# Attention with a gated mixture of experts: rows, K, Q and V in natural order at the begin, 44 unread products, the third group's loads moved ahead

## The reference

```python
def _L0_xattn_ref(q, k, v, mask, Wq, bq, Wk, bk, Wv, bv):   # 16 heads of 16
    Qh, Kh, Vh = split(q @ Wq + bq), split(k @ Wk + bk), split(v @ Wv + bv)
    scores = jnp.einsum('bqhd,bkhd->bhqk', Qh, Kh) / jnp.sqrt(jnp.float32(10.0))
    scores = jnp.where(mask[:, None, None, :] == 0, jnp.float32(-1000000000.0), scores)
    return jnp.einsum('bhqk,bkhd->bqhd', jax.nn.softmax(scores, axis=-1), Vh).reshape(B, S, D)
x = x + jnp.tanh(g_xattn[0]) * _L0_xattn_ref(_layernorm(x), ctx_1024, ctx_1024, mask, ...)
x = x + jnp.tanh(g_ffn[0]) * _L0_ffn_ref(_layernorm(x), Wg, W1, W2, W3)
```

## Time and profile before

| | |
|---|---|
| median of 3 runs | 827.55 us (827.4 to 828.44) |
| the profiled execution: its time | 823.12 us |
| its span, first to last instruction | 821.4 us |
| TensorE (PE) busy | 754.5 us, 92% |
| VectorE (DVE) | 564.9 us, 69% |
| ScalarE (ACT) | 513.2 us, 62% |
| GpSimd (POOL) | 368.7 us, 45% |
| mean granted TensorE clock | 0.960 |

### The profile page before, as it was taken

The page is one execution under the profiler, slowest core; times in us unless marked ns, Lnnn a source line. Parts: engine busy times, 40 slices in busy tenths (PEclk is TensorE's granted clock), DMA queues, the critical chain, the costliest instruction groups (busy, mean ns, idle before and its releaser), DMA issues. The chain is left out here.

```text
span 821.4 us, 24913 instructions
## 1 busy us (share of the span) xinstructions
PE 754.5 (92%) x9614; PEld 630.9 (77%) x9614; DVE 564.9 (69%) x1450; ACT 513.2 (62%) x1001; POOL 368.7 (45%) x761
## 2 busy tenths in 40 slices
PE   6799999999999999999998712999999999999995
PEld 3688888888888888888886601678889898888985
DVE  7577787778777877788778798584754747374440
ACT  3366777777777777767756675456565555656632
POOL 6233534453435443544322230627465474847416
PEclk8999999999999999999999955999999999999998
DMA  5543335543554345444332270535445363524314
GB/s 185 153 132 119 126 101 174 172 153 114 159 173 156 124 146 175 142 142 139 129 113 83 79 208 25 159 112 82 115 81 117 66 135 113 89 46 86 34 20 52
DMA packets 76773, 97.08 MB, mean 118 GB/s; under 512 B 8264, under 2 KB 55880, under 8 KB 76616
## 3 DMA queue, kind: packets, MB, share of 16 engines
q1 hardware_dynamic: 63120, 77.52, 29.5%
q0 software_dynamic: 12288, 17.05, 12.8%
q10 hardware_dynamic: 1248, 0.92, 0.3%
HBM read 52.37 MB, written 25.72 MB: 95 GB/s over the span
## 5 line engine op out<-in xcount | busy, mean ns | idle before, releaser
L746 DVE TENSOR_REDUCE m_sb<-a_ps 128x4 f32<-128x512 f32 x256 | 164.3, 684 | 53.2 <-PE a_ps L1047 51.6
L569 ACT ACTIVATE p_t<-b_ps 128x512 f32<-128x512 f32 x252 | 141.8, 589 | 66.0 <-PE b_ps L1055 63.7
L1047 PE MATMUL a_ps<-k_st,q_st 31*128 31x128 f32 x2048 | 148.7, 283 | 7.1 <-DVE m_sb L746 3.1
L1466 POOL DMA_INDIRECT out<-y,idx_add x64 | 100.4, 1569 | 114.5 <-ACT y L1527 93.2
L1047 PEld LDWEIGHTS a_ps<-k_st,q_st 31*128 31x128 f32 x2048 | 124.8, 186 | 32.3 <-issue 23.5
L1055 PE MATMUL b_ps<-q_st,k_st 32*128 32x128 f32 x1984 | 143.8, 283 | 0.0
L482 POOL TENSOR_TENSOR x<-o_n,x_res 128x256 f32<-128x256 f32 x63 | 46.3, 735 | 186.9 <-DVE o_n L836 168.5
L1055 PEld LDWEIGHTS b_ps<-q_st,k_st 32*128 32x128 f32 x1984 | 120.2, 186 | 0.0
L1727 DVE TENSOR_TENSOR act_h<-act_h,bank 128x512 f32<-128x512 f32 x64 | 44.0, 688 | 80.3 <-PE bank L1871 77.5
L1871 PE MATMUL bank<-x_hi,w_hi 128*128 128x512 f32 x248 | 97.6, 394 | 0.4 <-ACT act_h L1515 0.4
L1871 PE MATMUL bank<-x_lo,w_hi 128*128 128x512 f32 x248 | 96.6, 390 | 0.0
(11 more groups left out here) (299 smaller groups left out, 1742.4 us busy)
## 6 DMA issues: line engine op xcount, KB each, us to landing
w<-in_w_t SPq DMA_DIRECT2D x24, 512.0 KB, 4.7
rows_scratch<-xg SPq DMA_DIRECT2D x16, 528.0 KB, 3.4
x_in<-in_x SPq DMA_DIRECT2D x16, 512.0 KB, 4.7
c_t<-in_ctx_t SPq DMA_DIRECT2D x16, 512.0 KB, 4.4
k_st<-k_val SPq DMA_DIRECT2D x64, 128.0 KB
q_st<-q_val SPq DMA_DIRECT2D x64, 128.0 KB, 2.4
x_res<-in_x SPq DMA_DIRECT2D x16, 512.0 KB, 3.8
out<-x SPq DMA_DIRECT2D x16, 512.0 KB, 3.3
```

The source lines that it names most:

```text
L569: act.activation(p_t[b.s % 2][:, 4 * r:4 * r + 4, :], ps[q % 2][:].rearrange("p (h s) -> p h s", s=P), ACT.Exp, scale=SCALE).then_inc(exp_ ...
L746: dve.tensor_reduce(m_sb[b.s % 2][:, 4 * q:4 * q + 4], a_ps[q % 2][:].rearrange("p (h s) -> p h s", s=P), AX_X, ALU.max).then_inc(max_done, 1)
L1047: mm = pe.matmul(a_ps[i][:, t * P:(t + 1) * P], q_st[p][r:r + A_K, t, tok], k_st[p][r:r + A_K, t, tok], start=True, stop=True)
L1466: pool.indirect_dma_start(out[:, :], bass.IndirectOffsetOnAxis(ap=idx_add[e % 2][:, st:st + 1], axis=0), y[st][:], None, compute_op=ALU.ad ...
```

## The change

It touches the begin of attention and the first group's four batches.

- TensorE: 44 unread products instead of 20; the first group's fronts in the order 0 to 7; then the second group's rows (fronts 0 and 1), to `b_ps`, which are free until the third batch. The first group's batches then make the second group's fronts 2 to 7, two each in the first three batches, none in the fourth but for the third group's front 0.
- VectorE: the first group's `c_lo` (`first_context_lo`), GpSimd's until now, behind the bias row; `xn_rest` ahead of `make_k`; the second group's `xn_rest` ahead of the loop, its `make_k` in the first batch, its `make_v` in the third. One of the two fills of `q_st` goes to GpSimd.
- ScalarE: the second group's `context_hi` ahead of `q_out`, its rows' scaling behind it, and its `xn_t_out` ahead of the loop. `q_out` of the first group waits for `k_done` too, since both count up the same `f_free`. The second group's `q_out` stand both in the second batch.
- GpSimd: `context_lo` of the second group ahead of the fill of `v_aug[1]`.
- SP: the second group's mask and the third group's x are issued ahead of `stack_k`, the third group's context and mask behind `stack_q`, instead of in the first batch.

```diff
-WARM = 20
+WARM = 44
...
         if first(g):
             return (f_ps, m_ps, a_ps[0], a_ps[1], b_ps[0], b_ps[1], pv_ps, o_ps)[u]
+        if second(g) and u < 2:
+            return b_ps[u]
         return f_ps
...
             mask_row(Group(0, 0, NG))
+            load_mask(Group(0, 1, NG))
+            load_x(Group(1, 0, NG))
             stack_k(Group(0, 0, NG))
             stack_q(Group(0, 0, NG))
-            load_mask(Group(0, 1, NG))
+            load_c(Group(1, 0, NG))
+            load_mask(Group(1, 0, NG))
...
-                    if first(g):
-                        load_c(g.on(2))
-                        load_x(g.on(2))
-                        load_mask(g.on(2))
                     residual(g)
...
                 pool.memset(k_st[p][:], 0.0).then_inc(s_ones, 1)
+            pool.memset(q_st[1][:], 1.0).then_inc(s_ones, 1)
...
-            context_lo(Group(0, 0, NG))
             ln1(Group(0, 1, NG))
+            context_lo(Group(0, 1, NG))
             pool.memset(v_aug[1][:], 0.0).then_inc(s_zero, 1)
-            context_lo(Group(0, 1, NG))
...
                     f_wait(g, 4 + m)
+                    if first(g):
+                        act.wait_ge(k_done, m + 1)
...
-            normalise(Group(0, 1, NG), range(GB))
+            context_hi(Group(0, 1, NG))
             for m in range(KD):
                 q_out(g, m)
-            context_hi(Group(0, 1, NG))
+            normalise(Group(0, 1, NG), range(GB))
+            for k in range(KD):
+                xn_t_out(Group(0, 1, NG), k)
...
+            def first_context_lo():
+
+                for k in range(KD):
+                    dve.wait_ge(ch_done, k + 1)
+                    dve.tensor_tensor(c_lo[0][:, k, :], c_t[:, k, :], c_hi[0][:, k, :].bitcast(F32), ALU.subtract).then_inc(cl_done, 1)
...
+            first_context_lo()
             weights_rest(0)
             stats(Group(0, 1, NG), range(GB))
             weights_rest(1)
+            for k in range(KD):
+                xn_rest(g, k)
             for m in range(KD):
                 make_k(g, m)
-            for k in range(KD):
-                xn_rest(g, k)
...
-            v_ones(1)
+            for k in range(KD):
+                xn_rest(Group(0, 1, NG), k)
...
-            for u in (2, 3, 0, 1, 4, 5, 6, 7):
-                if u == 0:
-                    pe.wait_ge(w["s_id"], 2)
+            pe.wait_ge(w["s_id"], 2)
+            for u in range(8):
                 front(Group(0, 0, NG), u)
+            for u in range(KD):
+                front(Group(0, 1, NG), u)
...
-                if b.j == 0 and first(g):
-                    front(g.on(1), 0)
-                front(g.on(1), 2 * b.j + 1)
+                if not first(g):
+                    front(g.on(1), 2 * b.j + 1)
+                elif b.j < 3:
+                    front(g.on(1), 2 * b.j + 2)
```

More of the change, by code:

```diff
@@ L279, in first, with second @@
         return 2 * g.k + g.p == 0
+    def second(g):
+        return 2 * g.k + g.p == 1
     def at_last(b, g, j):
@@ L629, in step @@
                 exp(b.back(2), 1)
-                if b.j == 0:
-                    if first(g):
-                        xn_t_out(f, 0)
+                if b.j == 0 and not first(g):
                     xn_t_out(f, 1)
-                if b.j == 2:
+                if b.j == 1 and first(g):
+                    q_out(f, 0)
+                if b.j == 2 and not first(g):
                     q_out(f, 1)
@@ L692, in _ @@
             dve.memset(warm[:], 0.0).then_inc(s_warm, 1)
-            for p in range(2):
-                dve.memset(q_st[p][:], 1.0).then_inc(s_ones, 1)
+            dve.memset(q_st[0][:], 1.0).then_inc(s_ones, 1)
             def stats(g, ts):
@@ L892, in step @@
                 maximum(b, 1)
-                if b.j == 0:
-                    if first(b.group):
-                        xn_rest(f, 0)
+                if b.j == 0 and not first(b.group):
                     xn_rest(f, 1)
-                if b.j == 1:
+                if b.j == 0 and first(b.group):
+                    make_k(f, 0)
+                if b.j == 1 and not first(b.group):
                     make_k(f, 1)
-                if b.j == 3:
+                if b.j == 2 and first(b.group):
+                    v_ones(1)
+                    make_v(f, 0)
+                if b.j == 3 and not first(b.group):
                     make_v(f, 1)
@@ L906, in step @@
                 if b.j == 0:
-                    make_k(f, 0)
+                    make_k(f, 1 if first(b.group) else 0)
                     stats(b.group.on(2), (0, 1))
@@ L911, in step @@
                 if b.j == 2:
-                    make_v(f, 0)
+                    make_v(f, 1 if first(b.group) else 0)
                 if b.j == 3:
@@ L995, in front @@
                     pass
+                elif second(g) and u < 2:
+                    pe.wait_ge(q_done, KD)
                 elif u == 0:
```

20 lines of the change are left out of this document (10 added, 10 removed).

## The result

| | before | after |
|---|---|---|
| median, us (runs) | 827.47 (4: 826.82 to 828.44) | 820.11 (4: 818.94 to 820.87) |
| ratio, 95% interval | | 0.9912, 0.9900 to 0.9925 |
| profiled execution, us (span) | 823.12 (821.4) | 819.81 (818.1) |
| first scores | 27.78 | 24.50 |
| fifth batch's scores | 54.87 | 47.62 |

A forecast was written before the change was run, and what follows sets the result against it. TensorE is full in attention's loop, so an earlier start carries through. First scores 4.5 us earlier plus 3.4 from the first four batches make 7.9, taken off the median 827.55: 819.7 us, range 815.5 to 823.5.

The forecast's parts named there:

- the walk: TensorE's new order stepped through in time: rows until 13.5, first scores at 23.3, fifth batch at 47.0 us.
- Part 1: LayerNorm's scales: c_lo moved off GpSimd ends a collision, so xn starts 2.0 us earlier, at 9.9; moved memset does nothing.
- Part 2: VectorE's queue at the begin: w_lo_k done at 12.15, xn_lo at 16.1, k_val at 17.6, before Q's second front ends.
- the rival sum of 7.7: Alternative to 7.9: w_lo_q and w_lo_v lose up to 0.2 us each against GpSimd's second scales; no chance given.
- Part 3: Unread products, 20 to 44: end at 12.46, hold TensorE 0.5 us, keep full clock for K, rows and Q.
- Part 4: TensorE's begin in the new order: first scores at 23.3 instead of 27.78, 4.5 us earlier; q_st's transfer ready at 23.0.
- Part 5: SP's queue: the moved loads go out without open waits, near 13.8, ahead of k_done; cost 0, bound 0 to 1.
- Part 6: First group's four batches: first scores to fifth batch takes 23.7 us instead of 27.09, 3.4 us gained.
- the chance of 0.12: Rival, first batches: TensorE's idle pieces let the clock fall again, gain only 5 to 6.5 us, some 822; chance 0.12.
- The loads' rival: Rival at the stacking: K's and Q's transfers queue behind x_in and c_t, scores 2 to 4 us later, about 823; chance 0.06.
- the gain was not taken back: Rival: SP's stacking or ScalarE's normalise sets the fifth batch at 53 or later, 826 to 827.5; chance 0.04.
- the products did not hold PE at half clock throughout: Slower case at the begin: the 44 products stay at half clock, first scores at 38.4, time 834.8; chance 0.04.

The follow-up runs named there:

- e1: After with 20 unread products instead of 44; median 820.74 us, ratio to before 0.9926.
- e9: After with K ahead of the rows on TensorE and k_val ahead of xn_lo on VectorE; median 821.63 us, ratio 0.9935.
- e10: e3 with 32 unread products instead of 44, measured on another chip; median 816.54 us, ratio to before there 0.9903.
- e3: After with the fill of q_st[1] back on VectorE; median 820.02 us, ratio to before 0.9922.
- e6: e3 with the first half of the first group's K laid out from ScalarE's queue instead of SP's; median 820.88 us, ratio 0.9923.
- e7: After with the first group's two c_lo subtractions back on GpSimd; median 821.65 us, ratio to before 0.9940.
- e4: After with the second group's mask and third group's x, context and mask loads at their old places; median 821.05 us, ratio 0.9928.
- e13: After's new batches behind before's begin (20 products, K first, old loads, subtractions and fills), on another chip; median 826.93 us, ratio 1.0036.
- e2: Before with 44 unread products and nothing else changed; median 827.83 us, ratio to before 1.0008.
- e5: After with the first group's four batches as in before, the new begin kept; median 824.95 us, ratio 0.9980.

## Why the prediction was right

The forecast held: 819.7 against 820.11, within its range. Two terms in it were mis-sized: the first scores' by 1.2 too much, the batches' by 0.6 too little. The second makes up for half of the first, and the two hang together: in the walk K's first front of the second group waits for xn_lo until 24.95, and since the scores come late, that wait is gone (the front starts at 25.59). Where PE does not wait for q_st, as in e1, e9 and e10, the wait is there (0.48) and the batches take 23.63 to 23.67, the 23.7 of the forecast. That the sum is off by 0.4 only is chance beyond that: the number of products at half clock alone moves the rows by up to 1.1 (12.43 in e3, 13.57 in e6).

- **Part 1, the scales: half right.** Predicted 2.0, measured 1.1 (xn at 10.77, not 9.9). "The q_st memset that moves to POOL does nothing for this" is the step that failed. It shifts the next fill to 6.74 to 8.53, and DVE's first step of the scales takes 1.18 in place of 0.17; e3 shows it by taking the move back. The step has one input, and POOL's instruction only writes. The line of the Trainium skill (SBUF — State Buffer, "Who interferes with whom") that the prediction used is about instructions with two inputs; the same section names `tensor_scalar` among those that can take both pairs of ports and then contend with GpSimd, and this step is one. The trace agrees: the four BATCH_NORM_AGGREGATE from 6.96 on, beside the same fill, take 0.38 together as they do in before. The miss cost hardly anything in the end: xn is ready at 12.84 and the last unread product starts at 12.67. The collision with c_lo was right (e7: three steps held, first scores 1.75 later).
- **Part 2, DVE's queue: right.** K, Q and V start at 13.81, 16.68 and 19.47 (walk: 13.5, 16.4, 19.25), without a gap, and k_val is done at 17.93 (17.6). w_lo_q takes 0.66 as before and w_lo_v 0.73 instead of 0.68, beside POOL's second set of scales, so the up to 0.2 each of the rival sum of 7.7 are not there.
- **Part 3, the products: right in its effect, its price too low.** The rows start at 12.99, not 12.46. The 7.25 that the sum starts from is where the last of before's 20 products starts (7.27 in its trace), not where it ends (7.64 in the prediction's first paragraph): that is 0.3. The other 0.2 is one more product at half clock. That the 44 are needed was not shown: e1, with 20, is 1.29 later on PE and 0.57 at the scores, with a median that can't be told apart, and e10, with 32, starts the rows 1.1 earlier and keeps the clock.
- **Part 4, the first scores: the larger miss.** Forecast 23.3, measured 24.50, so 3.3 us instead of 4.5. On PE's path the second group's rows are done at 23.84 (22.78 + 1.06), 0.54 late, which is the late start of 12.99; then PE waits 0.66 for q_st. On the transfer's path "2.9 us behind the second q_val's end" was 4.14. q_val ended 0.26 late (20.36 and not 20.1), the stacking took 1.24 more (0.73 the long issue, 0.5 SP still issuing K's), and the forecast had 0.3 of slack: 0.26 + 1.24 - 0.3 = 1.2. The sum has no term for either. e10, where no issue is long, has its first scores at 22.68.
- **Part 5, SP: right about the loads, blind to the long issue.** e4 shows that they don't hold the stacking; the cost of 0 holds. That the new batches lose when x_in is late (0.7 in e4, 3.4 and the clock in e13) was not in the prediction.
- **Part 6, the batches: right, 0.6 low by the wait for xn_lo.** 23.12 instead of 23.7, and 23.67 in e10. The wait for DVE is 0.83 (0.8 forecast); ACT normalises at 41.5 to 43.6 (40.9 to 43.0 forecast), and its exponentials hold PE 0.55 and 0.47, together 1.0 where 1.6 was given back.
- **Sum.** 7.25 us at the fifth batch, 7.36 in the median, forecast 7.9: the loop carries the begin's gain through. Taking before's median as the base was needed; the difference of the two spans would have said 3.3.
- **The clock.** It did not fall in after. It did in e2 (PE idle 1.54, then 1.41), in e5 (1.98, then 1.41) and in e13 (4.22 at once), all near the first scores or behind them, as in before (0.80, then 1.41). One piece of 1.67 ahead of Q did not bring it down (e2 and e9, clock 1.00), nor 1.30 ahead of the rows (e10), nor after's 0.66, 0.83, 0.55 and 0.47. One outcome can't say whether the chance of 0.12 was right; without the second group's rows ahead of the scores the clock did fall (e5).
- **The loads' rival** fell with e4; the gain was not taken back, and the products did not hold PE at half clock throughout.

## What to carry to other kernels

When a begin becomes shorter, look at what fills the pause behind it: here the new batches keep the clock for the new begin, and neither is worth much alone (1.7 us gained and 3.0 lost by the ratios of e5 and e13, 7.3 gained together). A forecast of a queue's transfers needs the issues that stand ahead of them in the queue, not only the instruction that makes their data. Before moving an instruction to an idle engine "for nothing", place it and everything behind it on that engine in time, and see which tiny step of a serial chain it will now cover. Compare medians of several executions; one profiled pair can differ by several us in a stage that was never edited.
